# An attention and mixture-of-experts block on one core: the causal mask of the maxima's scores made inside the score product

## The chip, the cores and the metric

One core of one Trainium2 chip. The metric is the device time of one execution in microseconds (us). The engines are TensorE (PE in the rows, its weight loads PEld), VectorE (DVE), ScalarE (ACT), GpSimd (POOL) and SyncE (SP); SP computes nothing here and only issues DMA transfers.

## The reference

The block takes x (4 batches, 512 tokens, 256 features). It applies a modulated layer norm, causal attention with 32 query heads and 8 key heads of 8 features, a gated residual, a second modulated norm, and a layer with 16 routed experts (4 a token) and a shared one. What matters here is the softmax over the past:

```
att = jnp.einsum('bhqd,bhkd->bhqk', q, k) / math.sqrt(HD)
mask = jnp.triu(jnp.ones((seqlen, seqlen), dtype=bool), k=1)
att = jnp.where(mask[None, None, :, :], -jnp.inf, att)
att = jax.nn.softmax(att, axis=-1)
```

## The kernel before

**Halves and blocks.** Attention runs in eight halves u = 0 to 7: batch u // 2, and 16 of the 32 query heads with 4 key heads. A half goes over ten blocks of 128 queries by 128 keys (`GROUPS`: query tile q with key tile q, then the earlier key tiles) and, within a block, over four key heads g. One such step is a slot.

**Two score computations.** The exponentials need the row maximum first. So scores are computed twice. `scores_for_max` (L597 to L614) computes them with queries on partitions, for all keys of a query tile; VectorE takes the maxima (`maxima`, L1310); PE turns them (`turn_max`, L650), GpSimd splits them into three bf16 parts (`split`), and SP writes the parts by `put_negm` (L392) into rows 72 to 74 of the query operand Q. `scores` (L628) then computes keys by queries with 75 rows, maxima already subtracted, ScalarE takes the exponential (L1033), GpSimd zeroes the future in the diagonal blocks (`mask`, L1147), and `weigh_values` (L639) multiplies with the values. The maxima of half u + 1 are computed while half u runs; those of half 0 stand before it.

**The operands.** Q[i] and K[i] (three buffers, `QBUF`) have 72 rows each: 3 x 3 combinations of high, middle and low bf16 parts of 8 features. The parts go by SP to DRAM (`store_keys`, `store_side`; `store_parts` does both for a batch) and come back in the other layout (`load_half`, L383 and L385). Rows 72 to 74 of K are ones.

**The mask before.** For each PSUM bank `scores_for_max` adds one product of a bf16 identity `ident_bf` with `mask_qk` (0, or -1e30 in the future) to the last 128 columns of every head in it (L612). Per half and bank it has 4 heads at q = 0, 2 at q = 1 and 1 at q = 2 and 3; two banks are a pair, and VectorE reads a pair at once. So there are 4 mask products of 512 columns, 8 of 256 and 32 of 128.

**What sets the order.** Every engine's queue is written out by hand in program order, with semaphores. PE's order is `half`: in each slot a score product; at g = 0 also `weigh_values` of an earlier block; then the pairs that `pairs_after` gives to the slot. Score products use two PSUM banks in turn, so one waits for the exponential of the tile two before it. SP's order: inputs, `store_keys` and `store_side` of batch 0, `load_half(0)`, the rest of batch 0, `store_parts(1)`, `load_half(1)`, `put_negm(0, 0)`, `store_parts(2)`, further `put_negm`; in half 0 `load_half(2)` and `store_parts(3)`; in the halves 1 to 5 `load_half(u + 2)` and behind it the transfers that bring the softmax's inverse sums back (`spread_inverse`, L418 and L421), for which `normalise` (L1324) waits. GpSimd waits at the end of half 0 for all of `store_parts(3)` (L1226).

Of the kernel before, what the change touches and what calls it, by code (L numbers as in the profile page):

```python
# [7 lines left out]
P = 128  # L8
# [24 lines left out]
KR = PR + PARTS  # L33
EPS = 1e-5
# [30 lines left out]
QBUF = 3  # L65
# [3 lines left out]
def adaln_block(nc, x, wq, wk, wv, wo, gate_t, up_t, down_t, shared_up_t, shared_down_t, c_t, wmod, out):  # L69
    q_rows = nc.dram_tensor("q_rows", (B, 2, PARTS, PARTS, HD, HH, TP), BF16, kind="Internal").ap()  # L70
# [9 lines left out]
    with ExitStack() as ctx:  # L80
# [9 lines left out]
        ident_bf = sb("ident_bf", [P, P], BF16)  # L90
        mask_qk = sb("mask_qk", [P, REP, P], BF16)
# [17 lines left out]
        def region(start):  # L109
# [44 lines left out]
        wmod_sb = take(DC, 6 * D)  # L154
        parts = [region(at_)(3, PARTS, T, dt=BF16) for at_ in (16384, 23552)]
# [60 lines left out]
            const_done silu_c mod_done mod_used gate_mm gate_rows gate_out gate_bc v_ones k_ones ln_stats ln_sdev xn_ready  # L216
            tr_done h_ready qkv_done qkv_high v_done res1 mid_done low_done low_first first_out warmed consts counted
# [8 lines left out]
        q_in = [sem(f"q_in{i}") for i in range(QBUF)]  # L226
        k_in = [sem(f"k_in{i}") for i in range(QBUF)]
# [129 lines left out]
        with nc.Block() as block:  # L357
            @block.sync
            def _(sp):
# [9 lines left out]
                def store_side(b, h, signal):  # L369

                    for n in range(PARTS):
                        sp.dma_start(q_rows[b, h, n].rearrange("j d m t -> (d m) j t")[:, :, 0:T],
                                     parts[b % 2][:, h, :, :]).then_inc(signal, 16)
# [61 lines left out]

                sp.wait_ge(s["low_first"], 1)
# [4 lines left out]
                sp.wait_ge(s["k_ones"], QBUF)  # L441
# [8 lines left out]
                load_half(1)  # L450
                put_negm(0, 0)
# [4 lines left out]
                for u in range(HALVES):  # L456
# [87 lines left out]
            def _(pe):  # L544
# [227 lines left out]
                pe.wait_ge(s["consts"], 1)  # L772
# [354 lines left out]
            def _(gp):  # L1127
# [54 lines left out]
                gp.wait_ge(s["k_ones"], QBUF)  # L1182
                gp.wait_ge(s["const_done"], 1)
                step(nc.gpsimd.tensor_copy(ident_bf[:, :], ident[:, :]))
                step(nc.gpsimd.memset(mask_qk[:, :, :], 0.0))
# [477 lines left out]
```

## Time and profile before

| | us |
|---|---|
| median of 3 runs | 739.91 (739.47 to 749.11) |
| the profiled execution | 740.02 |
| its span | 738.3 |
| PE busy | 629.9 (85%) |
| DVE busy | 397.8 (54%) |
| POOL busy | 336.9 (46%) |
| ACT busy | 309.0 (42%) |

The span is what the engines' instructions cover; the execution's own time is 1.7 us longer. Matmuls are pipelined and their ends are modelled, so a busy PE is not PE at its peak. A chain of waits follows the work that ended last back in time, at each step to what released it. A row of a timeline has start, length, engine, line, operation, output and inputs, count, and in brackets the idle time before it with its releaser; the DMA rows (SPq) give the time of the issue, not of the transfer. A window gives, for each engine, busy time and number of instructions, then the granted PE clock as a share of 2.4 GHz, the mean busy share of the 16 DMA engines and what they moved.

### The profile page before, as it was taken

How to read it: one execution, taken by the hardware profiler on the slowest of the kernel's cores; microseconds unless marked ns; L12 is line 12 of the kernel's file. 1: busy time of each engine (PE TensorE's matmuls, PEld its weight loads, DVE VectorE, ACT ScalarE, POOL GpSimd, SP SyncE). 2: the span in 40 equal slices, each digit the busy share in tenths (PEclk: the TensorE clock that was granted, in tenths of full speed). 3: DMA queues.
4: the chain of work that ended last, by engine and by line, in shares of the span. 5: the costliest groups of instructions: out<-in, count | busy, mean ns of one | idle time of the engine just before them, and what ended most of it. 6: DMA issues, size and time to landing. Idle time of an engine off the chain costs nothing.

```text
span 738.3 us, 11493 instructions
## 1 busy us (share of the span) xinstructions
PE 629.9 (85%) x3376; PEld 349.1 (47%) x3384; DVE 397.8 (54%) x740; ACT 309.0 (42%) x660; POOL 336.9 (46%) x440
## 2 busy tenths in 40 slices
PE   8958799899999999999948606987999999999930
PEld 5434433333443343335323305564777777776720
DVE  5557567677788778876836115711333333333317
ACT  2421367667576757675712013212333333333300
POOL 5013353545254525453574740531665665665640
PEclk8979789999999999999968857998999999999975
DMA  7566219464132414120235970443666666766657
GB/s 236 165 212 188 79 27 331 132 195 94 39 80 53 94 38 84 49 51 3 46 125 136 390 230 4 168 161 87 103 111 106 107 111 108 111 112 99 103 102 282
DMA packets 82264, 91.41 MB, mean 124 GB/s; under 512 B 12122, under 2 KB 75578, under 8 KB 82046
## 3 DMA queue, kind: packets, MB, share of 16 engines
q1 hardware_dynamic: 65582, 69.28, 32.6%
q0 software_dynamic: 14448, 19.31, 15.9%
q10 hardware_dynamic: 2176, 2.10, 0.8%
q8 instruction: 30, 0.49, 0.3%
q14 instruction: 28, 0.23, 0.1%
HBM read 47.63 MB, written 42.63 MB: 122 GB/s over the span
## 4 chain that ended last, share of the span: by engine, by line
PE 55%; DMA 17%; DVE 10%; another core or an unknown queue 6%; issue 3%; SPq 3%; ACT 3%; POOL 2%; POOLq 0%; DVEq 0%; ACTq 0%
PE bank L892 10%; PE bank L910 7%; PE bank L639 6%; PE bank L608 6%; PE bank L628 6%; DMA y_inverse<-inverse 5%; DMA y_sum<-arena 4%; PE bank L827 3%; DMA q_rows<-arena 3%; PE bank L808 3%; PE bank L612 3%; DMA arena<-y_inverse 2%; DVE negm L1310 2%; PE bank L880 2%
## 5 line engine op out<-in xcount | busy, mean ns | idle before, releaser
L1033 ACT ACTIVATE arena<-bank 128x512 f32<-128x512 f32 x320 | 181.5, 599 | 113.2 <-PE bank L628 92.6
L1310 DVE TENSOR_REDUCE negm<-bank 128x2 f32<-128x1024 f32 (+3 forms) x176 | 192.5, 1120 | 65.3 <-PE bank L612 65.2
L1245 POOL DMA_INDIRECT y_sum<-arena x79 | 123.2, 1560 | 100.0 <-DVE arena L1609 88.0
L1147 POOL TENSOR_SCALAR_AFFINE_SELECT arena<-arena 128x512 f32<-128x512 f32 x128 | 81.2, 645 | 128.4 <-ACT arena L1033 124.9
L608 PE MATMUL bank<-arena 72*128 72x512 bf16 (+3 forms) x512 | 115.3, 308 | 13.4 <-ACT arena L944 7.4
L628 PE MATMUL bank<-arena 75*128 75x512 bf16 x320 | 116.2, 394 | 2.2 <-DVE arena L1316 0.6
L892 PE MATMUL bank<-arena 128*128 x316 | 109.9, 471 | 0.3 <-issue 0.3
L639 PE MATMUL bank<-arena 128*9 128x512 f32 x640 | 87.1, 617 | 11.1 <-ACT arena L1033 9.3
L1239 POOL DMA_INDIRECT x_rows<-arena,slots x64 | 63.7, 995 | 59.9 <-DVE slots L1459 41.2
L612 PE MATMUL bank<-mask_qk,ident_bf 128*128 128x128 bf16 (+2 forms) x344 | 84.8, 247 | 0.0
L910 PE MATMUL bank<-arena 88*128 x316 | 81.2, 379 | 0.0
L1602 DVE TENSOR_TENSOR arena<-bank,arena 128x176 f32<-128x176 f32 x79 | 27.1, 343 | 97.5 <-ACT arena L1106 95.4
L1106 ACT ACTIVATE arena<-bank 128x176 f32<-128x176 f32 x79 | 25.1, 318 | 129.6 <-PE bank L892 129.6
L608 PEld LDWEIGHTS bank<-arena 72*128 72x128 bf16 x512 | 49.4, 102 | 54.0 <-DVE negm L1310 20.0
L628 PEld LDWEIGHTS bank<-arena 75*128 75x128 bf16 x320 | 30.8, 99 | 92.3 <-ACT arena L1033 74.2
L892 PEld LDWEIGHTS bank<-arena 128*128 128x128 f32 x316 | 59.1, 193 | 25.7 <-issue 6.1
L1609 DVE TENSOR_SCALAR arena<-bank,arena 128x256 f32<-128x256 f32 x79 | 38.3, 485 | 59.1 <-PE bank L910 46.1
L910 PEld LDWEIGHTS bank<-arena 88*128 88x128 f32 x316 | 53.6, 190 | 4.5 <-issue 0.2
L808 PE MATMUL bank<-arena 128*128 128x512 f32 (+1 forms) x96 | 46.5, 626 | 5.6 <-issue 5.6
L612 PEld LDWEIGHTS bank<-mask_qk,ident_bf 128*128 128x128 bf16 x352 | 35.1, 100 | 11.9 <-issue 1.0
L880 PE MATMUL bank<-ident,arena 128*128 128x128 f32 x158 | 31.7, 283 | 4.6 <-DMA arena<-x_rows 4.4
L880 PEld LDWEIGHTS bank<-ident,arena 128*128 128x128 f32 x158 | 20.9, 143 | 29.0 <-issue 11.7
(169 smaller groups left out, 617.3 us busy)
## 6 DMA issues: line engine op xcount, KB each, us to landing
arena<-x_rows SPq DMA_DIRECT2D x79, 136.5 KB, 2.5
q_rows<-arena SPq DMA_DIRECT2D x24, 384.0 KB, 4.3
arena<-q_rows SPq DMA_DIRECT2D x8, 1152.0 KB
arena<-up_t SPq DMA_DIRECT2D x2, 2816.0 KB
arena<-y_sum SPq DMA_DIRECT2D x8, 512.0 KB, 7.1
arena<-down_t SPq DMA_DIRECT2D x2, 1408.0 KB
x_rows<-arena SPq DMA_DIRECT2D x17, 136.5 KB
k_rows<-arena SPq DMA_DIRECT2D x24, 96.0 KB, 2.9
```

The source lines that it names most:

```text
L608: nc.tensor.matmul(bank[:, buf + j, c * n:c * n + n], Q[k][0:PR, head, q * P:q * P + P], K[k][0:PR, head // REP, 0:n], start=(c == 0), sto ...
L612: last = nc.tensor.matmul(view[:, :, n - P:n], ident_bf[:, :], mask_qk[:, 0:heads, :], start=False, stop=True, skip_group_check=True)
L628: nc.tensor.matmul(bank[:, score_bank(u, tile), :], K[k][0:KR, g, kt * P:kt * P + P], Q[k][0:KR, g * REP:g * REP + REP, q * P:q * P + P], ...
L639: last = nc.tensor.matmul(bank[32 * g:32 * g + VW, OBANK, :], V[:, b * QT + kt, h * GH + g, :], probs[:, (NG * u + n) % SLOTS, g, :], star ...
L808: last = nc.tensor.matmul(bank[0:w, 2 * k + i, :], ws_up[:, c, c0:c0 + w], h2T[n][:, c, :], start=(c == 0), stop=(c == DC - 1))
L880: last = nc.tensor.transpose(bank[:, t % 2, c * P:c * P + P], xt[t % XT][:, c * P:c * P + P], ident[:, :])
L892: last = nc.tensor.matmul(bank[:, 2 + t % 2, 0:2 * I], xT[t % 2][:, c, :], w[:, bass.ds(e * (DC * 2 * I) + c * 2 * I, 2 * I)], start=(c == ...
L910: last = nc.tensor.matmul(bank[:, 6 + t % 2, 0:D], actT[t % 2][0:I2, c, :], w[0:I2, bass.ds(e * D, D)], start=(c == 0), stop=(c == 1))
L1033: nc.scalar.activation(probs[:, group % SLOTS, g, :], bank[:, score_bank(u, tile), :], ACT.Exp, scale=SCALE).then_inc(s["st_free"], 1)
L1147: nc.gpsimd.affine_select(out=block_, in_=block_, compare_op=ALU.is_ge, fill=0.0, base=0, pattern=[[0, REP], [1, P]], channel_multiplier=- ...
L1245: gp.indirect_dma_start(y_sum[t % 2], bass.IndirectOffsetOnAxis(ap=xt[t % XT][:, D:D + 1].bitcast(U32), axis=0), yo[t % YO], None, compute ...
L1310: nc.vector.tensor_reduce(to, view, AX.X, ALU.max, negate=True).then_inc(s["s_free"], 1)
```

## The change

The mask becomes part of the score product of the last 128 columns. Q and K get 43 more rows (`KR` = 75 to `MR` = 118). Each of these rows stands for three keys; the query side holds a negative power of two, by how far the query lies before the row's keys, or 0; the key side holds a positive power in the columns of its three keys. Their product is far below any score for a key in the future, and at most a small fraction otherwise. GpSimd builds one 128 x 128 tile of each side and copies it into Q[0] and K[0]; SP spreads it to the other heads and to the other two buffers (`spread_masks`). Rows 72 to 74 take part in this product too, so the query side must hold zeros there until `put_negm` writes them: `q_rows` gets 75 rows a half, three of them zero, and `load_half` loads 75 rows. K's ones are made with its mask rows. PE's program has, for each head, one product of the earlier keys with 72 rows (not at q = 0) and one of the last 128 keys with 118 rows.

```diff
+ROW_KEYS = 3
+MR = KR + -(-(P - 1) // ROW_KEYS)
+MASK_Q = (-2.0 ** 93, -2.0 ** 46, -0.5)
+MASK_K = (2.0 ** -62, 2.0 ** -15, 2.0 ** 32)
...
-    q_rows = nc.dram_tensor("q_rows", (B, 2, PARTS, PARTS, HD, HH, TP), BF16, kind="Internal").ap()
+    q_rows = nc.dram_tensor("q_rows", (B, 2, KR, HH, TP), BF16, kind="Internal").ap()
...
-                    sp.dma_start(Q[i][0:PR, :, :],
-                                 q_rows[b, h].rearrange("n j d m t -> (n j d) m t")[:, :, 0:T]).then_inc(q_in[i], 16)
+                    sp.dma_start(Q[i][0:KR, :, :], q_rows[b, h, :, :, 0:T]).then_inc(q_in[i], 16)
...
+                def spread_masks(i):
+
+                    if i == 0:
+                        sp.wait_ge(s["mask_rows"], 2)
+                        sp.dma_start(Q[0][KR:MR, 2:HH, :].rearrange("p (a m) t -> p a (m t)", m=2),
+                                     Q[0][KR:MR, 0:2, :].rearrange("p m t -> p (m t)").unsqueeze(1).to_broadcast(
+                                         [MR - KR, HH // 2 - 1, 2 * T])).then_inc(mask_in[0], 16)
+                        return
+                    sp.wait_ge(mask_in[0], 16)
+                    sp.dma_start(Q[i][KR:MR, :, :], Q[0][KR:MR, :, :]).then_inc(mask_in[i], 16)
+                    sp.dma_start(K[i][PR:MR, :, :], K[0][PR:MR, :, :]).then_inc(mask_in[i], 16)
...
+                spread_masks(0)
+                for j in range(PARTS):
+                    sp.dma_start(q_rows[:, :, PR + j, :, 0:T].rearrange("b h m t -> (b h) m t"),
+                                 zero_bf).then_inc(s["zero_out"], 16)
                 sp.wait_ge(s["low_first"], 1)
                 store_keys(0, 0, s["first_out"])
...
-                sp.wait_ge(s["k_ones"], QBUF)
+                sp.wait_ge(s["zero_out"], 16 * PARTS)
                 load_half(0)
...
                 load_half(1)
+                spread_masks(1)
                 put_negm(0, 0)
...
                         load_half(2)
+                        spread_masks(2)
                         store_parts(3)
...
+                        if u < QBUF:
+                            pe.wait_ge(mask_in[k], 32 if k else 16)
...
-                            nc.tensor.matmul(bank[:, buf + j, c * n:c * n + n], Q[k][0:PR, head, q * P:q * P + P],
-                                             K[k][0:PR, head // REP, 0:n], start=(c == 0), stop=False,
-                                             skip_group_check=True)
-                        view = bank[:, buf + j, 0:heads * n].rearrange("p (i n) -> p i n", i=heads)
-                        last = nc.tensor.matmul(view[:, :, n - P:n], ident_bf[:, :], mask_qk[:, 0:heads, :],
-                                                start=False, stop=True, skip_group_check=True)
+                            at_ = c * n
+                            if q > 0:
+                                nc.tensor.matmul(bank[:, buf + j, at_:at_ + n - P], Q[k][0:PR, head, q * P:q * P + P],
+                                                 K[k][0:PR, head // REP, 0:n - P], start=(c == 0), stop=False,
+                                                 skip_group_check=True)
+                            last = nc.tensor.matmul(bank[:, buf + j, at_ + n - P:at_ + n],
+                                                    Q[k][0:MR, head, q * P:q * P + P],
+                                                    K[k][0:MR, head // REP, q * P:q * P + P],
+                                                    start=(q == 0 and c == 0), stop=(c == heads - 1),
+                                                    skip_group_check=True)
...
-                pe.wait_ge(s["consts"], 1)
                 pe.wait_ge(s["h_ready"], DC * B)
...
-                for i in range(QBUF):
-                    above(gp, s["k_ones"], i)
-                    nc.gpsimd.memset(K[i][64:96, :, :], 1.0).then_inc(s["k_ones"], 1)
...
+                nc.gpsimd.tensor_copy(Q[0][top:P, 0:2, :].rearrange("p m (t n) -> p (m t) n", n=P),
+                                      mask_q[top:P, :].unsqueeze(1).to_broadcast([top, 2 * QT, P])
+                                      ).then_inc(s["mask_rows"], 1)
...
+                nc.gpsimd.tensor_copy(K[0][top:P, :, :].rearrange("p g (t n) -> p (g t) n", n=P),
+                                      mask_k[top:P, :].unsqueeze(1).to_broadcast([top, GH * QT, P])
+                                      ).then_inc(s["mask_rows"], 1)
```

## Rows read from the trace of the kernel before

**Rows 1.** Chain of waits: shares of the span by engine.

```profile
PE 55%; DMA 17%; DVE 10%; another core or an unknown queue 6%; issue 3%; SPq 3%; ACT 3%; POOL 2%; POOLq 0%; DVEq 0%; ACTq 0%
```

**Rows 2.** Costliest groups: shapes, count, busy us, mean ns, idle before; the mask product.

```profile
L612 PE MATMUL bank<-mask_qk,ident_bf 128*128 128x128 bf16 (+2 forms) x344 | 84.8, 247 | 0.0
```

**Rows 3.** Chain of waits in order of time: start us, length us, what.

```profile
86.79 0.43 PE bank L612
...
89.99 0.43 PE bank L628
...
209.51 0.06 PE bank L612
```

**Rows 4.** Timeline of PE, the eighth block of half 3 (n = 7).

```profile
222.46 0.39 PE L628 MATMUL bank<-arena 75*128 75x512 bf16 x1
222.69 0.38 PE L608 MATMUL bank<-arena 72*128 72x512 bf16 x1
...
223.77 0.38 PE L608 MATMUL bank<-arena 72*128 72x512 bf16 x1
...
224.52 0.39 PE L628 MATMUL bank<-arena 75*128 75x512 bf16 x1
```

**Rows 5.** Timeline of ACT, the same block.

```profile
222.89 0.60 ACT L1033 ACTIVATE arena<-bank 128x512 f32<-128x512 f32 x1 [0.64 <-PE bank L628]
...
223.86 1.74 ACT L1033 ACTIVATE arena<-bank 128x512 f32<-128x512 f32 x3
```

**Rows 6.** The same half: timelines, chain, landing times and waits around y_inverse.

```profile
215.34 0.84 SPq L383 DMA_DIRECT2D arena<-q_rows  x1
...
218.78 7.44 DMA y_inverse<-inverse
...
231.42 0.39 PE L608 MATMUL bank<-arena 72*128 72x512 bf16 x1 [0.98 <-DVE negm L1310]
...
DMA to landing us min/median/max: 1.5/7.7/7.7
...
DVE arena L1324 <- DMA arena<-y_inverse: 7.6, 5, 1.8
```

**Rows 7.** Timelines of SP, POOL and PE around the end of half 0.

```profile
106.92 0.86 SPq L383 DMA_DIRECT2D arena<-q_rows  x1
...
125.79 0.33 POOL L1226 MEMSET arena<- 128x273 f32 x1 [10.64 <-DMA q_rows<-arena]
...
134.99 1.05 PE L639 MATMUL bank<-arena 128*9 128x512 f32 x8 [0.51 <-POOL arena L1147]
```

**Rows 8.** Windows: us, busy time by engine, PE clock, DMA share, GB/s.

```profile
16.00:20.00 4.00, 4.00 (x7) 1.75 (x8) 1.14 (x2) 1.59 (x3) 0.00 (x0) 0.75 0.00 0
85.00:90.00 5.00, 4.78 (x25) 2.90 (x25) 1.41 (x2) 2.28 (x4) 3.54 (x9) 0.50 0.01 2
118.00:126.00 8.00, 7.94 (x59) 3.33 (x59) 6.00 (x6) 5.64 (x10) 0.21 (x1) 1.00 1.06 366
126.00:130.00 4.00, 3.62 (x27) 1.68 (x25) 3.02 (x5) 2.94 (x6) 3.62 (x11) 1.00 0.92 390
205.00:208.00 3.00, 3.00 (x28) 1.43 (x23) 2.48 (x4) 2.36 (x5) 2.08 (x6) 1.00 0.41 50
219.00:224.00 5.00, 5.00 (x34) 1.81 (x31) 4.56 (x7) 3.47 (x8) 3.82 (x8) 1.00 0.84 179
```

**Rows 9.** Timelines of SP and PE before half 0.

```profile
20.86 1.30 SPq L366 DMA_DIRECT2D k_rows<-arena  x3
...
28.65 0.98 SPq L383 DMA_DIRECT2D arena<-q_rows  x1
...
44.99 0.58 PE L608 MATMUL bank<-arena 72*128 72x128 bf16 x4 [7.36 <-ACT arena L944]
...
84.50 1.01 PE L628 MATMUL bank<-arena 75*128 75x512 bf16 x2 [0.58 <-DVE arena L1316]
```

**Rows 10.** Timeline of POOL: the memsets of K's rows of ones.

```profile
1.57 5.51 POOL L1181 MEMSET arena<- 32x2048 bf16 x3
```

More of the change, by code:

```diff
@@ L154, in adaln_block @@
         wmod_sb = take(DC, 6 * D)
+        mask_q, mask_k = (take(P, dt=BF16) for i in range(2))
+        zero_bf = take(T, dt=BF16)
         parts = [region(at_)(3, PARTS, T, dt=BF16) for at_ in (16384, 23552)]
@@ L215, in adaln_block @@
         names = """norm2 y_mm added norm_st norm_mv centred inverse_sd spread2 rows_turned turned w_in wm_in wg_in c_in wo_in
[L216 to L217 removed]
+            const_done silu_c mod_done mod_used gate_mm gate_rows gate_out gate_bc v_ones mask_q mask_k mask_rows mask_in0 mask_in1 mask_in2 zero_out ln_stats ln_sdev xn_ready
+            tr_done h_ready qkv_done qkv_high v_done res1 mid_done low_done low_first first_out warmed counted
             s_ready s_free st_ready st_free av_done o_free misc_ready misc_free nm_split y_ready x2_ready
@@ L226, in adaln_block @@
         q_in = [sem(f"q_in{i}") for i in range(QBUF)]
+        mask_in = [s["mask_in0"], s["mask_in1"], s["mask_in2"]]
         k_in = [sem(f"k_in{i}") for i in range(QBUF)]
@@ L371, in store_side @@
                     for n in range(PARTS):
-                        sp.dma_start(q_rows[b, h, n].rearrange("j d m t -> (d m) j t")[:, :, 0:T],
+                        sp.dma_start(q_rows[b, h, n * PR // PARTS:(n + 1) * PR // PARTS].rearrange(
+                                         "(j d) m t -> (d m) j t", j=PARTS)[:, :, 0:T],
                                      parts[b % 2][:, h, :, :]).then_inc(signal, 16)
@@ L1178, in _, with masked @@
                 gp.wait_ge(s["const_done"], 1)
-                for i in range(QBUF):
-                    above(gp, s["k_ones"], i)
-                    nc.gpsimd.memset(K[i][64:96, :, :], 1.0).then_inc(s["k_ones"], 1)
[L1182 to L1185, printed above, removed]
-                nc.gpsimd.affine_select(out=mask_qk[:, :, :], in_=mask_qk[:, :, :], compare_op=ALU.is_ge,
-                                        fill=NEG, base=0, pattern=[[0, REP], [-1, P]],
-                                        channel_multiplier=1).then_inc(s["consts"], 1)
+                def masked(to, signal, count, **how):
+                    nc.gpsimd.affine_select(out=to[:, :], in_=to[:, :], **how).then_inc(s[signal], 1)
+                    gp.wait_ge(s[signal], count)
@@ new lines, in _ @@
+                past = 1 - ROW_KEYS * KR
+                nc.gpsimd.memset(mask_q[:, :], MASK_Q[0]).then_inc(s["mask_q"], 1)
+                gp.wait_ge(s["mask_q"], 1)
+                for i in range(2):
+                    masked(mask_q, "mask_q", 2 + i, compare_op=ALU.not_equal, fill=MASK_Q[1 + i], base=-past - i,
+                           pattern=[[1, P]], channel_multiplier=-ROW_KEYS)
+                masked(mask_q, "mask_q", 4, compare_op=ALU.is_ge, fill=0.0, base=past + 1, pattern=[[-1, P]],
+                       channel_multiplier=ROW_KEYS)
@@ new lines, in _ @@
+                top = P // 2
+                nc.gpsimd.tensor_copy(Q[0][top:P, 0:2, :].rearrange("p m (t n) -> p (m t) n", n=P),
+                                      mask_q[top:P, :].unsqueeze(1).to_broadcast([top, 2 * QT, P])
+                                      ).then_inc(s["mask_rows"], 1)
+                gp.wait_ge(s["mask_rows"], 1)
+                nc.gpsimd.memset(mask_k[:, :], 0.0).then_inc(s["mask_k"], 1)
+                gp.wait_ge(s["mask_k"], 1)
+                for i in range(ROW_KEYS):
+                    masked(mask_k, "mask_k", 2 + i, compare_op=ALU.not_equal, fill=MASK_K[i], base=-past - i,
+                           pattern=[[1, P]], channel_multiplier=-ROW_KEYS)
@@ new lines, in _ @@
+                masked(mask_k, "mask_k", 5, compare_op=ALU.is_ge, fill=1.0, base=-KR, pattern=[[0, P]],
+                       channel_multiplier=1)
+                nc.gpsimd.memset(zero_bf, 0.0).then_inc(s["mask_k"], 1)
+                gp.wait_ge(s["mask_k"], 6)
+                nc.gpsimd.tensor_copy(K[0][top:P, :, :].rearrange("p g (t n) -> p (g t) n", n=P),
+                                      mask_k[top:P, :].unsqueeze(1).to_broadcast([top, GH * QT, P])
+                                      ).then_inc(s["mask_rows"], 1)
@@ L1189, in _ @@
+                gp.wait_ge(s["mask_rows"], 2)
                 step(nc.gpsimd.memset(minus_half[:, :], -0.5))
```

2 lines of the change are left out of this document (removed).

## The prediction

> **What bounds the kernel now.** I read the chain of waits first: TensorE (PE) carries 55% of it [rows 1]. The mask product at L612 is busy 84.8 us over 344 records [rows 2], but that busy time is modelled and overlaps its neighbours, so it isn't its price. The price is the step to the next instruction in the chain of waits: 0.43 us for 512 columns at a granted clock of 0.50, 1.2 GHz, and 0.06 us for 128 at 1.00, 2.4 GHz [rows 3, 8], so 0.11 for 256 and 0.22 for 512, as the step from 222.46 to 222.69 shows for a score product [rows 4]. One half (8192 mask columns: 4 of 512, 8 of 256, 32 of 128) therefore holds 4 x 0.22 + 8 x 0.11 + 32 x 0.06 = 3.6 us of masks.
>
> PE isn't the only limit, though. Take the block in [rows 4]: from the product at 222.46 to the one at 224.52 pass 2.06 us, of which PE needs three score products (0.22 each) and two pairs (0.55 each, a pair being two score products for the maxima with their masks), 1.76 us. The rest goes unseen under a busy figure of 0.39. ScalarE explains it [rows 5]: it starts an exponential 0.43 us after its product; then the copy out of PSUM and the next exponential follow 0.49 us apart, the latter at 223.86; score banks rotate by two, so the product at 224.52 waits until that one is through.
>
> Once a half there is a longer chain [rows 6]: SP issues the 1.44 MB load of a later half at 215.34, the small y_inverse store behind it takes 7.44 us and lands at 226.2 (10.9 us after the load's issue; alone such a store lands in 1.5), it is fetched back, VectorE normalises, and PE has waited 0.98 us at 231.42. VectorE's wait for it comes five times, once in each half with a load. Before them stands one more, at the end of the first half [rows 7]: SP issues load and stores from 106.92, GpSimd's memset (L1226) waits 10.64 us for the last store, until 125.79, and its masks then release PE at 134.99.
>
> **Part by part.** *TensorE.* Splitting off the last 128 columns leaves 8192 fewer columns a half and 4 more instructions, free at this pace. More rows in a product don't lengthen it (a 75-row product of 512 columns takes 0.23, a 128-row one of 128 columns 0.06 [rows 3, 4]). ScalarE needs 1.09 us from a block's second score product to its fourth (0.43 to start, 0.58 the exponential, 0.08 to release). A block with two pairs and no copy, such as the tenth, steps 1.86 us from its second score product to the next block's; now that is 1.09 + 0.22 + 0.44 = 1.75. Likewise, block by block: the first block of a half saves 0.74 us of its 0.88; the second, third and eighth (with a copy out of PSUM) nothing; fourth and fifth 0.12 each, sixth 0.24, seventh 0.14, ninth and tenth 0.11 each: 1.6 of 3.6 us. Where the y_inverse chain rules, only what precedes its anchor counts: 0.74 + 0.11 = 0.85 us a half.
>
> *Before the first half* (44.99 to 84.50 [rows 9]) the masks are worth 1.7 us at the low clock and 2.7 at the high one; VectorE's reductions follow closely, so I keep 2.6 (bounds 1.3 and 3.5). The part of the first half that precedes its anchor has 2.6 us, mostly at the low clock; I keep 2.0 (1.3 to 2.6).
>
> *GpSimd.* Removed: three memsets of 2048 columns, 5.51 us [rows 10], and three short steps. Added: twelve short steps and two copies of 1024 and 2048 columns, at the memset's 0.9 us a thousand columns or at twice that 2.8 to 5.5 us. Ready by 13 us at the latest; the next that waits for this queue is SP, whose next issue is at 20.86 [rows 9]. Cost 0; were that cover gone, some 2 us.
>
> *The load of a half* grows from 72 to 75 rows, see below.
>
> *The new transfers on SP's queue.* First what the windows show [rows 8]: with 128-row transfers the DMA share is 1.06; while only the 72-row load runs it is 0.84, 12.7 of 16 engines; with the 8-row y_values stores 0.41, 6.2 engines, with gaps between issues. So rows are dealt out in equal shares: 72 rows on 12 engines, 8 on 8. 43 is prime: equal shares leave **one** engine. The K part has 46 rows: two engines. 75 rows: 15.
>
> The Trainium skill (DMA: Bandwidth & Descriptors, "Why a DMA increments its semaphore by 16 and not by 1") states the rule: the largest number up to 16 that divides the slowest dimension of both sides; the three windows agree, and no run here shows one engine.
>
> An engine's rate: 390 GB/s at share 0.92 are 26.5 GB/s each [rows 8]. The first spread (43 x 14 KB, 616 KB) takes 23.3 us; each of the other two 704 KB, 26.6 us, and K on that same engine 94 KB, 3.6 us: 30.2 us. Upper bound: the 1 KB packets of the load, 179 GB/s at 0.84, 13.3 GB/s, so twice as long; lower bound: all engines at 366 GB/s, 2.4 us. I take 26.5, since these rows are long like those of that window. Later transfers on all 16 engines need that engine too, and wait behind, as y_inverse waits behind the load [rows 6].
>
> **Times.** (1) The queue is empty from 16 us on [rows 8]. The first spread holds its engine from about 15 to 38.3; behind it that engine has 24 + 90 packets of 1 KB, 5.4 us at the 21.6 GB/s of a share of 1.06, and a transfer lands 1.5 us later at best [rows 6]. So the first stores are in at 45.2, where the load was issued at 28.65 [rows 9]. It lands 9.7 us later (10.9 as in [rows 6], less the 1.2 of (4)), at 54.9: PE starts there, not at 44.99, **+9.9**. (2) SP then issues what it has before the load of half 1 and waits for the stores: that load goes out at about 60 and ends 9.7 us later, the second spread at 99.9. The negated maxima of the first half are queued behind it and land at 101.4; without them PE would start the half at 84.5 + 9.9 - 2.6 = 91.8. The next ones lie behind a batch's stores as well (180 KB an engine, 8.3 us) and land at 109.7. The second block waits for them; it started at 89.99 [rows 3], 16.9 us before the anchor at 106.92, of which masks take 0.9. The anchor moves to 125.7. (3) From there the last store landed 18.8 us later; now 18.8 - 1.2 + 30.2 = 47.8, at 173.5 instead of 125.79: **+47.7**. PE itself also waits for the third spread, which lands 9 us sooner and is covered by this. One microsecond more for a restart at the low clock. (4) The 1.2: on 15 engines instead of 12 each carries 16 fewer 1 KB packets, 16 x 77 ns at the load's 13.3 GB/s an engine. Bounds: 0.3 us longer (5% more bytes, if the rate isn't the engines'). It shortens each of the five chains: -1.3 in the first, four times 0.85 + 1.2, -8.2, and the last two halves -1.9: **-11.4**.
>
> Sum against the profiled execution (740.02 us, span 738.3; the median 739.91 is the same): 740.0 + 47.7 + 1.0 - 11.4 = 777.3; forecast **777 us**. What comes later (weights load, experts) starts after attention and moves with it. This case's own range is 757 to 820: down, an engine 10% faster (6 us on two spreads) and 14 us for what SP may get out earlier than I have it and the bounds above; up, spreads a third slower (20 us on two, some 8 on the first) and 15 for the rest.
>
> **Rivals.** *A, the small cost (735.6 us, not slower), 0.13.* The spreads run on all engines like the 128-row stores. Then 0.89 MB before the stores at 108 us cost 3.9 us at their 230 GB/s (4.3 MB in 18.8 us), +0.2 for the load; -4.6 before the anchor leaves -0.5, the five chains -2.0 with the load 0.3 longer, the end -1.9: 735.6. For it: nothing in the trace runs on one engine. Against: the 0.84 window. It decides if the 43 rows keep more than about ten engines busy. *B, PE is all, 0.02.* Every mask column counts (8 x 3.6 and 2.6 more at the low clock, with free spreads): 709. Against it: the unseen 0.3 us in [rows 4]. *C, a slow engine, 0.05.* At 13.3 GB/s spreads take 46 and 60 us: the first shifts PE by 33, the second ends at about 153 and moves the anchor to 179, the last store lands 77.6 us on, at 257: 861 us. *My case, one engine at full rate: 0.80.*
>
> The range 757 to 820 leaves out A, B and C, 0.20 together. A change within 2% (14.8 us) is about what counts as none here. Slower: my case and C, 0.85; within 2%: A, 0.13; faster: B, 0.02.
>
> **What would show it.** Right: DMA share near 0.06 for some 20 to 30 us three times (about 16 to 38, 70 to 100, 135 to 165 us), PE idle before its first score product until about 55 us and before the first half until about 101, GpSimd's memset waiting tens of microseconds, blocks two, three and eight of a half unchanged (3.4 us apart). The load then has a share near 1.0. Wrong: shares of 0.8 or more in the spreads, or masks landing before the loads.

## The result, and the profile after

The changed kernel takes 790.91 us in the median of four runs (790.15 to 792.47), the kernel before 743.36 (739.47 to 749.11, four runs on the same chip): a ratio of **1.069 (95%: 1.064 to 1.075)**, slower. The profiled execution took 791.43 us with a span of 789.7; it stands against the 740.02 us and 738.3 of the profile before, 51.4 us more. The forecast was 777 us, range 757 to 820.

What answers to [rows 8]: windows of the changed kernel (us, busy time by engine, PE clock, DMA share, GB/s).

```profile
16.00:24.00 8.00, 8.00 (x36) 4.74 (x36) 3.76 (x6) 5.05 (x9) 0.00 (x0) 0.90 0.07 28
...
90.00:100.00 10.00, 0.37 (x1) 0.09 (x1) 2.49 (x4) 1.84 (x3) 1.36 (x4) 0.64 0.16 60
150.00:155.00 5.00, 0.00 (x0) 0.00 (x0) 0.00 (x0) 0.00 (x0) 0.00 (x0) 0.50 0.06 26
...
195.00:200.00 5.00, 4.87 (x38) 1.75 (x35) 4.49 (x7) 4.21 (x8) 2.22 (x5) 1.00 0.89 205
```

One sixteenth is 0.0625. At 16 to 24 us and at 150 to 155 us one DMA engine moves 26 to 28 GB/s, and in the second window no computing engine does anything. In the window at 90 to 100 us the second spread has company (0.16); in its first half, 90 to 95 us, the share is 0.07 too, at 29 GB/s. The 75-row load (195 to 200 us) now shows 0.89, 14.2 of 16 engines, and 205 GB/s, where the 72-row one had 0.84 and 179.

SP's timeline of the changed kernel: the first spread (L401), the zero stores (L459), the first stores (L375, L381), the first load (L393); then the third spread (L406, L407) and the stores of the last batch.

```profile
8.82 0.88 SPq L401 DMA_DIRECT2D arena<-arena  x1
9.75 24.18 SPq L459 DMA_DIRECT2D q_rows<-arena  x3
33.97 2.49 SPq L375 DMA_DIRECT2D k_rows<-arena  x3
...
45.84 0.92 SPq L393 DMA_DIRECT2D arena<-q_rows  x1
...
128.91 0.93 SPq L393 DMA_DIRECT2D arena<-q_rows  x1
...
130.72 0.68 SPq L406 DMA_DIRECT2D arena<-arena  x1
131.45 0.63 SPq L407 DMA_DIRECT2D arena<-arena  x1
132.12 13.38 SPq L375 DMA_DIRECT2D k_rows<-arena  x3
145.54 20.02 SPq L381 DMA_DIRECT2D q_rows<-arena  x3
```

The slow transfer doesn't only delay what is queued behind it: SP itself stands still in the middle of issuing. Three stores of zeros take it 24.18 us, six stores of batch 3 another 33.4. The kernel has no wait between the three stores; a single one of them took 21.6 us to issue (duration in ns, min/median/max):

```profile
L459 SPq DMA_DIRECT2D q_rows<-arena x3: 1234/1240/21618, 9.8 to 32.7; - x3
```

What answers to [rows 9] and [rows 7], timelines of PE and POOL:

```profile
56.08 1.86 PE L642 MATMUL bank<-arena 118*128 118x128 bf16 x16 [18.46 <-DMA arena<-k_rows]
...
105.03 1.01 PE L661 MATMUL bank<-arena 75*128 75x512 bf16 x2 [11.55 <-DMA arena<-arena]
...
112.94 1.03 PE L661 MATMUL bank<-arena 75*128 75x512 bf16 x2 [4.12 <-DMA arena<-arena]
...
176.53 0.33 POOL L1279 MEMSET arena<- 128x273 f32 x1 [39.38 <-DMA q_rows<-arena]
```

PE starts its maxima at 56.08 instead of 44.99, the first half at 105.03 instead of 84.50, and GpSimd's memset is released at 176.53 instead of 125.79.

For all kernels below I use the same few places, as starts in us of each profiled execution. "Cut" means that every transfer of mask rows is split in two, "whole" that it is left as in the changed kernel; "inverse first" means y_inverse issued ahead of the load. "Six halves" is the distance from the first to the seventh of VectorE's normalising products (L1324 before, L1377 after); the last column is the issue of the experts' weight load.

| kernel | ratio to before (95%) | first maxima | load of half 2 | memset | first normalise | six halves | weight load |
|---|---|---|---|---|---|---|---|
| before | 1 | 45.0 | 106.9 | 125.8 | 156.2 | 219.7 | 400.4 |
| changed | 1.069 (1.064 to 1.075) | 56.1 | 128.9 | 176.5 | 206.8 | 211.0 | 443.0 |
| e1, transfers cut | 0.985 (0.976 to 0.994) | 44.8 | 103.2 | 127.5 | 157.9 | 209.2 | 390.4 |
| g1, first whole | 1.001 (0.995 to 1.008) | 56.3 | 115.5 | 139.7 | 170.3 | 210.4 | 406.3 |
| e2, third whole | 1.026 (1.017 to 1.035) | 45.2 | 104.7 | 152.8 | 183.5 | 209.4 | 419.1 |
| f1, third whole, late | 1.061 (1.051 to 1.070) | 56.1 | 129.0 | 147.3 | 213.7 | 210.0 | 438.5 |
| e3, no mask | 1.005 (0.998 to 1.013) | 41.7 | 101.6 | 120.3 | 151.0 | 219.2 | 394.9 |
| e4, e1 with 72-row loads | 1.007 (1.002 to 1.013) | 44.8 | 103.2 | 127.4 | 158.7 | 215.5 | 400.5 |
| e5, before with 75-row loads | 0.988 (0.978 to 0.999) | 44.8 | 107.9 | 126.4 | 156.2 | 215.1 | 394.3 |
| v1, e1, inverse first | 0.988 (0.981 to 0.995) | 46.3 | 105.9 | 130.6 | 159.7 | 207.4 | 390.0 |
| v2, before, inverse first | 0.994 (0.988 to 1.000) | 44.7 | 106.6 | 125.9 | 155.0 | 217.3 | 396.9 |
| v3, v1, third spread late | 0.985 (0.979 to 0.991) | 45.3 | 104.8 | 123.0 | 159.6 | 208.5 | 386.5 |
| v4, e5, inverse first | 0.986 (0.981 to 0.991) | 44.8 | 108.1 | 126.2 | 155.4 | 216.4 | 388.8 |

The ratios compare fast executions alone (one of f1's four took 1526 us and is left out), while the profiles of e1 and g1 are of slow ones, so I use only their times up to the weight load. f1, v3 and v4 ran on another chip, where the kernel before takes 705.66 us instead of 740 to 747; their ratios are to that.

### The profile page after: what moved, and what is told of

Its sections match the earlier page's. It is cut to its first block, busy times and chain, and to the rows that moved or that the text cites. A ratio compares the mean times of both kernels' runs of the same rounds, so it can differ in the third digit from the quotient of the medians.

```text
span 789.7 us, 11585 instructions
## 1 busy us (share of the span) xinstructions
PE 616.0 (78%) x3416; PEld 346.4 (44%) x3416; DVE 398.4 (50%) x740; ACT 308.4 (39%) x660; POOL 334.2 (42%) x446
## 4 chain that ended last, share of the span: by engine, by line
PE 37%; DMA 23%; SPq 12%; DVE 8%; issue 7%; another core or an unknown queue 5%; ACT 4%; POOL 3%; DVEq 0%; POOLq 0%; ACTq 0%
PE bank L924 7%; PE bank L942 6%; PE bank L672 6%; DMA arena<-arena 5%; PE bank L661 5%; DMA y_inverse<-inverse 4%; DMA y_sum<-arena 4%; DMA arena<-x_rows 4%; SPq L459 3%; ACT arena L1065 3%; SPq L381 3%; DMA arena<-y_inverse 2%; PE bank L639 2%; DVE negm L1363 2%
## 5 line engine op out<-in xcount | busy, mean ns | idle before, releaser
L661 PE MATMUL bank<-arena 75*128 75x512 bf16 x320 | 121.7, 399 | 22.8 <-DMA arena<-arena 15.7
L642 PE MATMUL bank<-arena 118*128 118x128 bf16 x512 | 85.3, 232 | 41.7 <-DMA arena<-arena 23.2
L924 PE MATMUL bank<-arena 128*128 x316 | 109.7, 470 | 0.3 <-issue 0.3
L672 PE MATMUL bank<-arena 128*9 128x512 f32 x640 | 89.3, 631 | 16.6 <-ACT arena L1065 10.2
L639 PE MATMUL bank<-arena 72*128 72x128 bf16 (+2 forms) x384 | 83.5, 279 | 5.7 <-DVE negm L1363 5.7
L642 PEld LDWEIGHTS bank<-arena 118*128 118x128 bf16 x512 | 49.4, 105 | 59.7 <-issue 46.0
L840 PE MATMUL bank<-arena 128*128 128x512 f32 (+1 forms) x96 | 48.4, 646 | 7.3 <-issue 7.3
L639 PEld LDWEIGHTS bank<-arena 72*128 72x128 bf16 x384 | 38.7, 101 | 29.5 <-DVE negm L1363 19.5
```

What stands on the lines that cost most here:

```text
L639: nc.tensor.matmul(bank[:, buf + j, at_:at_ + n - P], Q[k][0:PR, head, q * P:q * P + P], K[k][0:PR, head // REP, 0:n - P], start=(c == 0), ...
L642: last = nc.tensor.matmul(bank[:, buf + j, at_ + n - P:at_ + n], Q[k][0:MR, head, q * P:q * P + P], K[k][0:MR, head // REP, q * P:q * P + ...
L661: nc.tensor.matmul(bank[:, score_bank(u, tile), :], K[k][0:KR, g, kt * P:kt * P + P], Q[k][0:KR, g * REP:g * REP + REP, q * P:q * P + P], ...
L672: last = nc.tensor.matmul(bank[32 * g:32 * g + VW, OBANK, :], V[:, b * QT + kt, h * GH + g, :], probs[:, (NG * u + n) % SLOTS, g, :], star ...
L924: last = nc.tensor.matmul(bank[:, 2 + t % 2, 0:2 * I], xT[t % 2][:, c, :], w[:, bass.ds(e * (DC * 2 * I) + c * 2 * I, 2 * I)], start=(c == ...
```

## The experiments

### One transfer at a time (m1)

```
rows(48, 75)   # b[75:123] <- a[75:123], 16 KB a row, then wait
rows(43, 75); rows(44, 75); rows(45, 75); rows(46, 72); ...
```

> This kernel computes nothing: SP sends copies of rows from one SBUF tile to another (16 KB a row, 4 KB in the last of them), one at a time, each waited for before the next is issued; then it copies x to the output. Counts of rows, in this order: 48, 43, 44, 45, 46, 47, 50, 128, 48, 32, 11, 72, 75 and last 46 of 4 KB. My theory (rows are dealt out in equal shares, so the number of engines is the largest up to 16 that divides the rows; 26.5 GB/s an engine, plus 1.5 us to land): 48 rows on 16 engines 3.4 us, 43 on one 28.1, 44 on eleven 4.0, 45 on fifteen 3.4, 46 on two 15.7, 47 on one 30.6, 50 on ten 4.6, 128 on sixteen 6.4, 32 on sixteen 2.7, 11 on eleven 2.1, 72 on twelve 5.2, 75 on fifteen 4.6, 46 rows of 4 KB on two 5.1. Rival (nothing is special about 43; what was slow was the company of other transfers): every copy takes 1.5 us and its bytes at one common rate, so 43, 44, 45, 46, 47 within 10% of each other.

Windows from one issue to the next (us, busy DVE and POOL, PE clock, DMA share, GB/s), for 48, 43, 44, 45, 46, 47, 50 and 128 rows:

```profile
9.42:17.09 7.67, 0.00 (x0) 0.00 (x0) 1.00 0.57 103
17.09:45.47 28.38, 0.00 (x0) 0.00 (x0) 1.00 0.06 25
45.47:52.85 7.38, 0.00 (x0) 0.00 (x0) 1.00 0.40 98
52.85:60.42 7.57, 0.00 (x0) 0.00 (x0) 1.00 0.52 97
60.42:77.13 16.71, 0.00 (x0) 0.00 (x0) 1.00 0.11 45
77.13:107.87 30.74, 0.00 (x0) 0.00 (x0) 1.00 0.06 25
107.87:116.16 8.29, 0.00 (x0) 0.00 (x0) 1.00 0.41 99
116.16:124.59 8.43, 0.00 (x0) 0.00 (x0) 1.00 0.80 249
```

43 rows take 28.38 us, 44 take 7.38. The rival with one common rate is out, and the three slow counts come where equal shares put them: 43 and 47 at a share of 0.06, 46 at 0.11, within 7% of the expected times. The Trainium skill ("DMA: Bandwidth & Descriptors", "Why a DMA increments its semaphore by 16 and not by 1") gives the engines as the largest number up to 16 that divides the slowest dimension on both sides; the shares of 0.06 and 0.11 agree. Those of the other counts, 0.40 to 0.80, are means with idle time in them and don't count engines. My times for many engines were all too short, though: 48 rows take 7.67 us and not 3.4, at 103 GB/s where 128 rows get 249; 11 rows take 4.49 (expected 2.1), 72 take 8.65 (5.2) and 75 take 8.83 (4.6). Sixteen engines take 48 rows in 7.67 us where one takes 43 in 28.38: 3.7 times as fast, not sixteen times. And 75 rows are not faster than 72 here, so the load's gain in the kernel can't be read off these copies.

### The same rows in two transfers (e1)

```diff
-    sp.dma_start(Q[i][KR:MR, :, :], Q[0][KR:MR, :, :])
-    sp.dma_start(K[i][PR:MR, :, :], K[0][PR:MR, :, :])
+    for lo, hi in ((KR, KR + 32), (KR + 32, MR)):
+        sp.dma_start(Q[i][lo:hi, :, :], Q[0][lo:hi, :, :])
+    for lo, hi in ((PR, PR + 32), (PR + 32, MR)):
+        sp.dma_start(K[i][lo:hi, :, :], K[0][lo:hi, :, :])
```

The first spread is cut in the same way.

> The changed kernel with the same mask rows and bytes in the same places of SP's queue, but each transfer of 43 rows cut into 32 and 11, and each of 46 (K) into 32 and 14. My theory (the number of engines is the cause): the three spreads nearly vanish; PE's first score product near 47 us, load of half 2 issued near 104, GpSimd's memset released near 124, and the end near the kernel before, 735 to 745 us, ratio to it 0.99 to 1.00. Rival 1 (the bytes and their place in the queue are the cause): 775 to 790, as before the cut. Rival 2 (the two products a score with their own weights, not the transfers, cost part of it): 750 to 770.

The ratio is 0.985 (0.976 to 0.994), against 1.069 whole: same rows, same bytes, same places in the queue. SP's timeline of the cut kernel: first spread, zero stores, first load, and the third spread with batch 3 behind it; then POOL's memset.

```profile
9.22 1.81 SPq L403 DMA_DIRECT2D arena<-arena  x2
11.08 3.79 SPq L463 DMA_DIRECT2D q_rows<-arena  x3
...
28.15 0.88 SPq L393 DMA_DIRECT2D arena<-q_rows  x1
...
104.95 1.44 SPq L409 DMA_DIRECT2D arena<-arena  x2
106.43 1.37 SPq L411 DMA_DIRECT2D arena<-arena  x2
107.85 2.26 SPq L375 DMA_DIRECT2D k_rows<-arena  x3
110.15 4.38 SPq L381 DMA_DIRECT2D q_rows<-arena  x3
...
127.50 0.33 POOL L1283 MEMSET arena<- 128x273 f32 x1 [16.07 <-DMA q_rows<-arena]
```

The zero stores take SP 3.79 us instead of 24.18, the same six of batch 3 6.6 instead of 33.4. The number of engines is the cause; both rivals are out. The gain is a little larger than expected (ratio 0.99 to 1.00, 735 to 745 us; measured 732.09), and the memset comes 3.5 us later than expected. What is left of the third spread is 127.50 - 103.20 = 24.3 us from the load to the last store, where it was 18.9: 5.4 us for 0.89 MB. The prediction had 3.9 for free spreads.

### One transfer left whole: the first (g1), the third (e2)

```diff
 # g1, in the cut kernel, for Q[0] only
-    for lo, hi in ((KR, KR + 32), (KR + 32, MR)):
+    for lo, hi in ((KR, MR),):
 # e2, in the cut kernel, for i == 2 only: the two whole transfers of the changed kernel
```

> The cut kernel with the first spread alone (43 rows, from head 2 on) left whole; the second and third are cut. It divides the 23.3 us that the changed kernel's first normalise is behind the one with only the third spread whole (206.8 against 183.5 us). Theory (the first stores wait for that one engine and everything until the end of the first half moves with them): first maxima's product near 56 us instead of 44.8, the first half's first score product near 94 instead of 82.7, load of half 2 near 114, first normalise near 169, and the time 10 to 12 us over the cut kernel (1.5% of it). Rival (VectorE's reductions or the later batches' stores have slack that takes it up): first maxima near 56 us, but load of half 2 before 108 us and less than 5 us in the end.

> As the kernel with the transfers cut, but the third spread (43 and 46 rows, issued behind the load of half 2) left whole. My theory: until the load of half 2 nothing differs from the cut one; then batch 3's stores wait on the one engine, its last store lands 28.8 us later than in the cut kernel (what the step from this load's issue to the last store grew by, from 18.87 to 47.62 us, in the changed kernel), and all of it reaches the end: cut kernel + 27 to 31 us, 762 to 775. The remaining 18 to 22 us of the changed kernel's loss belong to the first two spreads. Rival (PE has slack there, or the delays overlap and only the longest counts): less than 15 us over the cut kernel.

In g1 the first maxima start at 56.28 us, the load of half 2 at 115.5, and the first normalise is 12.4 us later than in the cut kernel (170.3 against 157.9). Ratio 1.001: 1.7% over the cut one, as expected. In e2 it is 25.7 us later (183.5). The last store lands 152.8 - 104.7 = 48.1 us after the load's issue, as in the changed kernel (47.6). The ratio 1.026 is 4.2% over the cut kernel's, the medians (757.42 and 732.09 us) 25 us apart. The rival (under 15 us) is out, but my 27 to 31 us are missed too: I had taken what the step grew by over the kernel before, 28.8 us, and the cut kernel already has 5.4 of that. The changed kernel is 49.0 us behind the cut one at this place; less g1's 12.4 and e2's 25.7, that leaves 10.9 for the second spread. This is a remainder: no kernel has the second spread alone whole, so that the three simply add up isn't shown. From the memset to the first normalise pass 30.4 us before, and 30.3, 30.4, 30.7 and 30.6 in the changed kernel, e1, e2 and g1: in all of them the last store sets the time.

### The third spread behind the stores (f1)

```diff
 # in the changed kernel
-    spread_masks(2)
     store_parts(3)
+    spread_masks(2)
```

> The changed kernel with its whole transfers of 43 and 46 rows; only the third spread is issued behind the last batch's stores instead of ahead of them. The prediction said that the last store rules there and that PE's own wait for the third spread, 9 us sooner, is covered. If that is all, the stores' land some 28 us earlier but PE waits for the spread itself, which now starts 13 us later: it lands near 174 instead of 165 us, GpSimd's memset is released near 148 instead of 176.5, and the last exponential weights' product of the first half's masks comes 0 to 8 us earlier than before: time 783 to 791 us. Rival 1 (only the stores' wait counts, the spread is hidden behind the first half): 760 to 768. Rival 2 (the negated maxima, one row each, queue behind the spread on its engine and hold the second half): 791 to 800.

Timelines of POOL and PE:

```profile
147.32 0.33 POOL L1279 MEMSET arena<- 128x273 f32 x1 [10.09 <-DMA q_rows<-arena]
...
181.87 1.01 PE L642 MATMUL bank<-arena 118*128 118x128 bf16 x8 [36.33 <-DMA arena<-arena]
```

The stores land 29 us earlier and the memset at 147.32, as expected; but PE then waits 36.33 us for the spread, until 181.87 (in the changed kernel until 168.7), and the first normalise comes at 213.7, 6.9 us **later**. The chain of waits has the spread at 40.0 us from its issue at 141.6, behind the stores; in the changed kernel, behind the load, at 37.0. I had expected 0 to 8 us earlier; the place it comes out at is rival 2's, though by the spread itself and not by the negated maxima. The time's ratio, 1.061 (1.051 to 1.070), was measured on the other chip and doesn't show these 6.9 us. As a ratio my 783 to 791 us are 1.058 to 1.069, so the time is as expected while the place is not. Moving a one-engine transfer hides nothing here: the next wait is PE's own.

### How much the mask is worth (e3, e4, e5)

```diff
 # e3, in the kernel before
-    last = nc.tensor.matmul(view[:, :, n - P:n], ident_bf[:, :], mask_qk[:, 0:heads, :], ...)
 # e4, in the cut kernel
-    sp.dma_start(Q[i][0:KR, :, :], q_rows[b, h, :, :, 0:T])
+    n_rows = KR if u < QBUF else PR
+    sp.dma_start(Q[i][0:n_rows, :, :], q_rows[b, h, 0:n_rows, :, 0:T])
 # e5, in the kernel before: q_rows with KR rows, three of them zero
-    sp.dma_start(Q[i][0:PR, :, :], ...)
+    sp.dma_start(Q[i][0:KR, :, :], q_rows[b, h, :, :, 0:T])
```

> The kernel before, with the mask product left out: the maxima are taken over unmasked scores, so this part of the computation is missing. It bounds what any cheaper mask on TensorE can bring. My theory (ScalarE's exponentials and the y_inverse chain cover most of it): 0.85 us in each of seven halves and 2.6 before the first, 8.5 us in all, so 731 us and a ratio near 0.989. Rival (PE is all, every mask column counts, 3.6 us in each of eight halves and 2.6): 709 us, ratio 0.958.

> The kernel with the cut mask transfers, but the loads from the fourth on bring 72 rows instead of 75 (twelve engines instead of fifteen). The three rows of the negated maxima are then not zeroed for the maxima's products of those halves, a part left out: they see the older maxima, and no instruction is saved on an engine. In the cut kernel a half takes 1.6 to 1.75 us less than in the kernel before (normalise at 157.9, 191.2, 227.3, 260.8, 297.1 us; before 156.2, 191.5, 229.5, 264.9, 302.7). Theory of the load (all of this comes from the 75-row load on fifteen engines, nothing from the masks, as the kernel without masks suggests, whose halves are as long as before's): from the fourth half on, halves as long as before, the last normalise some 8 us later than in the cut kernel, the time 6 to 9 us longer than its 732. Rival (the prediction's: masks 0.85 us, load 0.8 us a half): half of that, 3 to 4 us.

> The kernel before with its mask product, but its loads bring 75 rows (the three rows of the negated maxima as zeros, stored once in the same way as in the changed kernel). Theory of the load: halves 1.6 to 1.75 us shorter than before in seven halves, the last normalise near 397 instead of 407.7 us, the time near 729 to 732. Rival (masks and load share the gain): 0.8 us a half, 734. Second rival (the load doesn't matter, only the masks): as before, 740.

e3: with no mask product at all the kernel isn't faster, 1.005 (0.998 to 1.013). "PE is all" (709 us) is out, but my 731 is missed as well. In the trace the first maxima start earlier (the first load went out at 25.5 instead of 28.7, which masks don't touch), and the first normalise comes 5.3 us earlier; then six halves take 219.2 us, as good as the 219.7 before, where I had expected 5 less. From a normalise to the next load's issue three of four distances are 0.8 to 0.9 us shorter, as expected; one is 0.6 longer, and from the load to the normalise the sum of five grew by 1.1. Why the chain takes this back I can't say.

After e3 I believed for a while that the masks give nothing and the load all. In the halves, e4 and e5 say otherwise. In six halves the 75-row load alone (e5) wins 219.7 - 215.1 = 4.6 us, the mask rows with 72-row loads (e4) 219.7 - 215.5 = 4.2, both (e1) 10.4. That is near the share rival: about half each, and 1.6 more together. It doesn't fit e3, where the product left out altogether gives 0.4; this stays open.

At the end of attention, and in the time, it looks otherwise. e4's last normalise is at 408.8 us, 9.7 behind e1's 399.1, where the theory of the load said 8 and the rival half of that; its ratio is 2.3 points over e1's, more than either expected. e5's last normalise is at 401.4 us, for which the theory said 397; in the time it has 0.988, and e4, with mask rows and without the load, has 1.007. So the load alone has nearly the ratio of the cut kernel (0.985), and the mask rows alone, whose cut transfers bring the first normalise 2.5 us later, show no gain.

The chain of waits shows the load's part, in half 3 of e4 (72 rows) and e5 (75 rows), beside 7.44 in [rows 6]:

```profile
219.69 7.91 DMA y_inverse<-inverse
```

```profile
218.25 6.53 DMA y_inverse<-inverse
```

### y_inverse ahead of the load (v1 to v4)

```diff
+    if u > 0:
+        spread_inverse(u - 1)
     if u > 0 and u + 2 < HALVES:
         sp.wait_ge(s["st_ready"], E_TOT * u)
         ...
         load_half(u + 2)
-    if u > 0:
-        spread_inverse(u - 1)
```

v1 is this in the cut kernel, v2 in the kernel before, v4 in e5. v3 is v1 with the (cut) third spread behind batch 3.

> The kernel with the cut mask transfers, and in each half with a load the small y_inverse transfers are issued ahead of the load instead of behind it. That takes the longest chain of a half away: its store should land in some 2 us instead of 6.8 to 7.7. Theory (that chain sets the length of a half, and masks on TensorE are worth what the block-by-block sum gave, 1.6 us a half, only without it): 1.6 to 3 us a half shorter than the cut kernel, 715 to 725 us. Rival (ScalarE and the maxima's reductions are right behind the chain): less than 0.5 us a half, 729 to 733. Second rival (the load, issued 4 to 5 us later, and the negated maxima behind it come too late): 740 or more.

> The kernel before with the same exchange: y_inverse ahead of the load, mask product and 72-row load kept. With the chain gone, the difference between this and the cut kernel with the exchange is what the mask rows are worth. Theory: 722 to 732 us here, and 5 to 12 us more than with the mask rows. Rival (masks are covered by ScalarE in every block): within 3 us of the one with mask rows. If the chain was no limit: 740.

> The cut kernel with y_inverse ahead of the load, and the third spread (cut) behind the last batch's stores. In the cut kernel the last store lands 24.3 us after the load of half 2 was issued, against 18.9 before the change: the spread ahead of the stores costs 5.4 us there. Theory: the memset is released 4 to 5 us earlier, but PE wants the masks of half 2 at about the same time, so 1 to 4 us are won over the cut kernel with y_inverse first, 722 to 733 us. Rival (PE waits for the masks instead): no gain or up to 3 us lost.

> The kernel before (mask product with the identity) with the two things that its timing took from the change or from the experiments, but without mask rows: loads of 75 rows, and y_inverse ahead of the load. Against the cut kernel with y_inverse first it differs by the masks alone. From the first to the last normalise the latter takes 237.5 us, the kernel before with y_inverse first and 72-row loads 249.0. Theory (masks are worth 1.6 us a half once the y_inverse chain is gone, and the load no longer matters): 247 to 249 us, time about 741. Rival (of the 11.5 us about half is still the load): 242 to 244 us, time about 736.

SP's and VectorE's timelines in v1:

```profile
251.84 0.33 SPq L443 DMA_DIRECT2D y_inverse<-inverse  x1
253.29 0.56 SPq L446 DMA_DIRECT2D arena<-y_inverse  x1
```

```profile
259.54 1.23 DVE L1367 TENSOR_REDUCE negm<-bank 128x2 f32<-128x1024 f32 x1 [1.00 <-PE bank L646]
260.68 0.69 DVE L1381 TENSOR_TENSOR arena<-arena 128x512 f32<-128x512 f32 x1
```

The store lands in 1.4 us instead of 6.8, and the chain is gone: VectorE comes to the normalise from a reduction, with no wait for y_inverse. But only 1.9 us are won in six halves (209.25 to 207.39): the rival, less than 0.5 us a half, is right, and the time (734.8 us in the median) is near its 729 to 733. v2 wins 2.4 us in six halves and takes 743.03 us, not 722 to 732; against v1 on the same chip it is 8.2 us longer, within the 5 to 12 of the theory. With no wait for y_inverse left, I take PE's and ScalarE's blocks to set the half, and there the masks can be read off. PE's first products of the blocks with values, v2 and v1:

```profile
281.69 1.05 PE L639 MATMUL bank<-arena 128*9 128x512 f32 x8
...
301.89 1.05 PE L639 MATMUL bank<-arena 128*9 128x512 f32 x8
305.73 1.05 PE L639 MATMUL bank<-arena 128*9 128x512 f32 x8
...
315.68 1.05 PE L639 MATMUL bank<-arena 128*9 128x512 f32 x8
```

```profile
273.79 1.05 PE L676 MATMUL bank<-arena 128*9 128x512 f32 x8
...
299.70 1.05 PE L676 MATMUL bank<-arena 128*9 128x512 f32 x8
302.82 1.05 PE L676 MATMUL bank<-arena 128*9 128x512 f32 x8
306.17 1.05 PE L676 MATMUL bank<-arena 128*9 128x512 f32 x8
```

Ten blocks take 33.99 us in v2 (281.69 to 315.68) and 32.38 in v1 (273.79 to 306.17): **1.6 us a half**, the number of the prediction's block-by-block sum. The first block gives 3.84 - 3.12 = 0.72 of it. v4 against v2 says that in six halves the load now gives 0.9 us (216.4 and 217.3) where it gave 4.6 with the chain in place. v4's own expectation was missed, though: from the first to the last normalise it takes 240.4 us, under the theory's 247 to 249 and the rival's 242 to 244. The difference is in the last distance, 24.0 us against 31.6 in v2. The chip explains it at least in part: v3, on v4's chip, has 25.6 there and v1 has 30.1, and v2's chain of waits has 14.1 us of "another core or an unknown queue" between 370.6 and 385.3 us, v4's none. The time of 741 was made for the other kind of chip.

v3 releases the memset at 122.98, but PE waits 8.0 us for the masks instead, until 129.33, and the first normalise stays at 159.6: the rival's no gain.

Five kernels have ratios 1.2 to 1.5% under the kernel before, inside the 2% that I called no change; for e1, e5 and v3 the interval reaches past 2%. v3 and v4 ran on the same chip: 694.91 and 696.77 us. The mask rows win 7.9 us in six halves (208.5 against 216.4, 1.3 a half) and give 4.2 back before the first normalise; at the weight load 2.3 are left, and in the time, next to v4, which has the 75-row load without them, no difference is shown.

## Why the prediction was right

The forecast was 777 us and the profiled execution took 791.4, inside the range. The mechanism held up to the weight load; one size agrees in part by luck, another was too large, and 8.8 us came where nothing was forecast.

**Engines.** Right. 43 rows run on one engine at 25 to 28 GB/s (predicted 26.5), 46 on two (a share of 0.11 in m1); the 75-row load's share of 0.89 fits fifteen and isn't the "near 1.0" that the prediction named as a sign.

**(1) First stores.** Load at 45.84 (predicted 45.2), PE at 56.08 (54.9). The step held, and one engine alone was indeed still busy at the end of it (42 to 44 us: share 0.07, 24 GB/s). That SP was stopped as well is not in the prediction: the stores went out at 33.97 us and not at about 21. As far as the prediction goes, it is luck that this moved the load by only 0.6 us.

**(2) Second spread.** Load of half 1 at 62.57 (60), first half at 105.03 (101.4), second block at 112.94 (109.7), anchor (the load of half 2) at 128.91 (125.7). The miss is 2.6 us at the load and hardly grows: the prediction had SP at that load a little early.

**(3) Third spread.** From anchor to memset 47.6 us (47.8). The last store is in at 176.5 (173.5), all of its +50.7 against +47.7 inherited from (2). That PE's own wait ends earlier and is covered is right too (168.7 against 176.5); f1 shows what it is worth when nothing covers it.

**(4) Masks and load.** Masks ahead of the anchor 0.85 us a half: measured 0.85 to 1.06 from normalise to load. Blocks, changed against before: first 3.12 against 3.84, second and third 3.36 and 3.43 against 3.39 and 3.43, fourth and fifth 0.10 less each, sixth 0.21, seventh 0.13, eighth 3.36 against 3.35, ninth 0.11. The table was 0.74; 0, 0; 0.12 each; 0.24; 0.14; 0; 0.11. The load was sized too large: 1.2 us predicted, while from its issue to the normalise the changed kernel is 0.5 to 0.7 us shorter than the kernel before, and e5 0.45 to 0.8. From the first normalise to the weight load the changed kernel regained 8.0 us (50.6 to 42.6), predicted 10.1; four loads at 0.6 instead of 1.2 make 2.4 us, about that miss. Also, the prediction's masks of one half, added up as printed, are 3.7 us and not 3.6.

**Sum.** 791.4 - 777.3 = 14.1 us: 3.2 by the first normalise, 2.1 regained less, and 8.8 after the weight load, where I had said that all moves together: that step of the prediction didn't come out. Those 8.8 aren't shown to be the change's. Two places carry most of them, SP's sixteen writes of pad rows and PE's waits for x_rows. SP's timelines of the pad writes, in the kernel before, in the changed one, and in e3, which has no mask rows:

```profile
467.84 27.70 SPq L514 DMA_DIRECT2D x_rows<-arena  x16
```

```profile
510.96 33.39 SPq L541 DMA_DIRECT2D x_rows<-arena  x16
```

```profile
462.65 32.56 SPq L514 DMA_DIRECT2D x_rows<-arena  x16
```

The costliest groups, PE's transposes of the experts' tokens with their waits, in the same order:

```profile
L880 PE MATMUL bank<-ident,arena 128*128 128x128 f32 x158 | 31.7, 283 | 4.6 <-DMA arena<-x_rows 4.4
```

```profile
L912 PE MATMUL bank<-ident,arena 128*128 128x128 f32 x158 | 31.5, 282 | 12.7 <-DMA arena<-x_rows 12.7
```

```profile
L877 PE MATMUL bank<-ident,arena 128*128 128x128 f32 x158 | 31.4, 282 | 11.3 <-DMA arena<-x_rows 11.3
```

e3 and e5 (32.71 and 12.6 us) have the long form of both without mask rows; e2, with them, has the short one (27.67 and 4.3 us). From the weight load's issue to the end, the profiles on chips of the first kind, without e1 and g1, take 334.4 (v1), 338.1 (e2), 340.0 (e4) and 346.7 us (changed) with mask rows, 337.9 (before), 338.7 (v2), 340.8 (e5) and 344.0 (e3) without. What picks the form stays open.

**Rivals.** A (small cost, 735.6 us) is what the cut kernel does: 732.09 us in the median. So A's time was near what its condition gives, and the condition, more than ten engines on the 43 rows, was what failed. Its stages don't all agree: e1's first normalise is at 157.9 us where A has 155.7, its weight load at 390.4 where A has 396.0. B fell with e3. C (13.3 GB/s) fell with m1: rows of 16 KB run at 25.

## What to carry to other kernels

Count the slowest dimension of every transfer: 43 rows took 28 us and 44 took 7, and a cut into 32 and 11 turned a ratio of 1.069 into 0.985. Such a transfer stops the queue that issues it too, and moving it behind the stores only made PE's own wait for it the longest. A cheaper product is worth what the block with the tightest limit lets through: of 3.6 us of masks a half, 1.3 to 1.6 with the longer chain gone, and with it in place 0.7 to 1.0 by e4 and e1, but 0.1 by e3. Look also at what comes along with a change: three more rows in the load gave by themselves a ratio of 0.988 (e5), next to the cut kernel's 0.985.

## What the runs showed of the hardware

- SP stops in its own issues while one DMA engine is behind: 24.18 us for three small stores behind 43 rows (one of them 21.6), 3.79 behind 32 and 11 rows.
- A transfer of few rows stays slow on many engines too: 48 rows of 16 KB at 103 GB/s, 32 rows in 4.59 us and 11 rows in 4.49; 72 rows in 8.65 us and 75 in 8.83.
- Chips differ by stage. The kernel before takes 740 to 747 us on one kind and 705.66 on another. Between the weight load's issue and the first pad write pass 61.8 to 68.4 us in ten profiles on the first kind and 38.8 to 40.2 in three (f1, v3, v4) on the other; the pad writes take 27.66 us or more and 21.05 to 21.36. The chain of waits says where: in the kernel before 44 us of it are "another core or an unknown queue", all after 370 us (26.81 in one piece, from 412.75 us, in which VectorE waits), and 4.7 to 6.3% of the span in the profiles of all ten kernels on the first kind; in the three on the other it has none. What releases these waits, and why the other chip has none, isn't shown. SP's timeline of v3:

```profile
386.54 6.40 SPq L536 DMA_DIRECT2D arena<-up_t  x2
...
426.72 21.05 SPq L545 DMA_DIRECT2D x_rows<-arena  x16
```
